# Last layer of a four-layer graph network: which operand of the dense product TensorE holds, and how the strips are loaded

## The reference

```python
def _L3_gnn_ref(emb, edge_weight, row, col, num_layers):
    w = edge_weight[:, None]
    X = emb
    for _ in range(num_layers):              # 3
        msgs = w * X[col]
        X = jax.ops.segment_sum(msgs, row, num_segments=n)
    return X
...
x = _layernorm(x + _L3_gnn_ref(x, edge_weight, src, dst, 3), axis=-1)
```

## Time and profile before

| | us |
|---|---|
| median of 3 runs | 4498.11 (4493.66 to 4520.53) |
| the profiled execution | 4511.84 |
| its span, first to last instruction | 4510.1 |
| mean granted clock of TensorE | 0.903 of full |
| last layer, from its first load to the end | 4060.9 to 4510.1 |

### The profile page before, as it was taken

One profiled execution on the slowest core, in us unless ns is written; L12 is line 12 of the kernel. 1 busy time (PEld: TensorE's weight loads), 2 busy tenths in 40 slices (PEclk: granted clock), 3 DMA queues, 4 the chain that ended last, 5 costly groups with the idle time before them and its releaser, 6 DMA issues. The chain is left out here.

```text
span 4510.1 us, 106688 instructions
## 1 busy us (share of the span) xinstructions
PE 3111.8 (69%) x28819; PEld 1977.5 (44%) x28820; DVE 2512.7 (56%) x7841; ACT 1512.7 (34%) x3455; POOL 2049.9 (45%) x3286
## 2 busy tenths in 40 slices
PE   2420000257777777777777799999999449988998
PEld 1100000046666666666665355555555325542222
DVE  7842212466666666666665698989998514440000
ACT  0011111124333333333333577777777301100000
POOL 1047777534444444444442588888888400000000
PEclk9999999879888888888887798988998779998999
DMA  9101111134444443334341110110101450008673
GB/s 375 58 14 23 22 23 22 20 107 136 136 135 135 135 135 121 127 120 129 120 136 70 28 27 26 26 27 26 28 26 26 85 106 0 0 0 367 287 303 136
DMA packets 190491, 431.03 MB, mean 96 GB/s; under 512 B 32352, under 2 KB 143066, under 8 KB 177274
## 3 DMA queue, kind: packets, MB, share of 16 engines
q1 hardware_dynamic: 156988, 365.02, 23.1%
q0 software_dynamic: 32816, 61.65, 6.1%
q10 hardware_dynamic: 520, 2.80, 0.2%
HBM read 227.36 MB, written 136.86 MB: 81 GB/s over the span
## 5 line engine op out<-in xcount | busy, mean ns | idle before, releaser
L208 POOL DMA_INDIRECT sorted_edges<-s_record,s_index x400 | 476.1, 1190 | 370.6 <-issue 362.1
L809 POOL TENSOR_TENSOR e_part<-e_rest,e_part 128x256 bf16<-128x256 f32 x202 | 133.2, 659 | 785.6 <-ACT e_part L851 785.6
L1016 DVE TENSOR_TENSOR e_strip<-e_p_aw,e_strip 128x256 f32 x804 | 334.9, 417 | 269.3 <-issue 199.7
L1347 POOL TENSOR_SCALAR m_oh<-m_iotab,m_rec 128x128 bf16<-128x128 bf16 x812 | 474.5, 600 | 0.1
L2068 PE MATMUL r_p_o<-r_W,r_X 128*32 128x512 f32 (+1 forms) x1050 | 408.3, 549 | 41.4 <-DMA r_W<-dense_strips 39.2
L803 POOL TENSOR_TENSOR e_ohw<-e_oh,e_rec 128x512 bf16<-128x512 bf16 x408 | 420.7, 1059 | 10.5 <-DVE e_oh L993 7.8
L1793 PE MATMUL q_p_s<-q_A,q_g 128*96 128x512 bf16 (+1 forms) x1750 | 349.5, 357 | 102.8 <-DMA q_A<-dense_strips 101.5
L259 PE MATMUL s_p_t<-s_ident,s_oh_src 125*128 125x125 f16 x100 | 21.2, 284 | 504.3 <-issue 259.0
L1000 DVE TENSOR_SCALAR e_ohw<-e_p_iota,e_rec 128x128 bf16<-128x128 f32 x816 | 327.7, 403 | 0.0
L842 ACT ACTIVATE e_hid<-e_p_hid,e_b 128x512 f32<-128x512 f32 x204 | 140.3, 688 | 557.8 <-PE e_p_hid L901 557.8
L1793 PEld LDWEIGHTS q_p_s<-q_A,q_g 128*96 128x96 bf16 x1750 | 197.7, 123 | 235.0 <-issue 105.8
(11 more groups left out here) (309 smaller groups left out, 7423.0 us busy)
## 6 DMA issues: line engine op xcount, KB each, us to landing
r_W<-dense_strips SPq DMA_DIRECT2D x18, 6400.0 KB, 17.7
e_strip<-e_zeros SPq DMA_DIRECT2D x26, 3200.0 KB, 13.8
dense_strips<-e_strip SPq DMA_DIRECT2D x25, 3200.0 KB
sorted_edges<-s_neg SPq DMA_DIRECT2D x1, 40560.0 KB, 161.8
e_rec<-sorted_edges POOLq DMA_DIRECT2D x208, 130.0 KB, 2.4
m_rec<-sorted_edges SPq DMA_DIRECT2D x208, 130.0 KB, 2.1
q_A<-dense_strips POOLq DMA_DIRECT2D x25, 800.0 KB, 46.2
sorted_edges<-s_record,s_index POOLq DMA_INDIRECT x400
```

The source lines that it names most:

```text
L208: pool.indirect_dma_start(dram["edges"], bass.IndirectOffsetOnAxis(ap=index[s][:, c:c + 1], axis=0), record[s][:, c, :], None).then_inc(s_ ...
L1016: i = V.tensor_tensor(at, p_aw[u][:, v, :].rearrange("p (k c) -> p k c", k=2), at, ALU.add)
L1347: i = g.tensor_scalar(oh[s][:, t, :], iotab[:, :], rec[s][:, t, CDST:CDST + 1], None, ALU.is_equal)
```

## The change

The operands of the product change places. A 128 by 128 block of a strip becomes TensorE's weights, and X, 32 columns, moves; the result comes out with the target nodes in the partitions, as X needs it. ScalarE's copies, the transposes, `r_Y` and its copy to X go; VectorE copies each group of four finished blocks from PSUM (seven tiles `r_p_o`, one for each group) right into the other of two X tiles. In step n+1 the matmul of source block d = 0, 4, 8, ... of the first strip waits for the copy of the group that it reads.

The buffers hold single strips now. Ten of the 25 strips (those with b % 5 of 2 or 4) have a buffer each and are loaded once, the other 15 pass through a ring of three in every step. TensorE waits for each strip alone. The loops over steps are written out on TensorE, VectorE and SP, and the flags go.

```diff
-        SL = 3
-        W = [sb(f"W{k}", [P, 4, NB, P]) for k in range(SL)] + [sb(f"W{SL}", [P, width[-1], NB, P])]
-        X = sb("X", [P, NB, D])
-        Y = sb("Y", [P, NB, D])
+        stays = [b % 5 in (2, 4) for b in range(NB)]
+        RING = 3
+        held = [sb(f"held{k}", [P, NB, P]) for k in range(sum(stays))]
+        ring = [sb(f"ring{k}", [P, NB, P]) for k in range(RING)]
+        passing = [b for b in range(NB) if not stays[b]]
+        order = [(n, b) for n in range(STEPS3) for b in passing]
+        X = [sb(f"X{k}", [P, NB, D]) for k in range(2)]
...
         def _(sp):
-            for f in primed:
-                sp.sem_inc(f.semaphore, 1)
-            with sp.Fori(1, STEPS3 + 1) as n:
-                for c in range(CH):
-                    last_user(sp, summed, slot, c, n)
-                    sp.dma_start(W[slot[c]][:, :, :, :].rearrange("p b d k -> p b (d k)"),
...
+            for n in range(STEPS3):
+                for b in range(NB):
+                    if stays[b] and n:
+                        continue
+                    strip, strip_in, _ = strip_of(n, b)
+                    if not stays[b]:
+                        i = order.index((n, b))
+                        if i >= RING:
+                            n0, b0 = order[i - RING]
+                            sp.wait_ge(multiplied, n0 * NB + b0 + 1)
+                    sp.dma_start(strip[:, :, :].rearrange("p d k -> p (d k)"), dram["strips"][b, :, 1, :]).then_inc(strip_in, 16)
...
         def _(pe):
...
-                    for d in range(NB):
-                        m = nc.tensor.matmul(p_o[c % 3][:, 0:width[c] * P], X[:, d, :],
-                                             W[slot[c]][:, :, d, :], start=(d == 0), stop=(d == NB - 1))
-                    summed[c].set_by(m)
-                    if c:
-                        turn(c - 1)
-                turn(CH - 1)
+            for n in range(STEPS3):
+                for b in range(NB):
+                    strip, strip_in, count = strip_of(n, b)
+                    pe.wait_ge(strip_in, count)
                     for d in range(NB):
+                        if b == 0 and d % 4 == 0:
+                            if n:
+                                pe.wait_ge(gathered, (n - 1) * CH + d // 4 + 1)
+                            elif d == 0:
+                                pe.wait_ge(started, 1)
+                        m = nc.tensor.matmul(p_o[b // 4][:, b % 4, :], strip[:, d, :], X[n % 2][:, d, :],
+                                             start=(d == 0), stop=(d == NB - 1), skip_group_check=True)
+                    m.then_inc(multiplied, 1)
...
-                    turned[c].after(dve, n)
-                    gathered[c].set_by(V.tensor_copy(Y[:, 4 * c:4 * c + width[c], :], p_t[c % 2][:, 0:width[c], :]))
-                gathered[CH - 1].after(dve, n)
-                renewed.set_by(V.tensor_copy(X[:, :, :], Y[:, :, :]))
+                    dve.wait_ge(multiplied, n * NB + 4 * c + width[c])
+                    V.tensor_copy(X[1 - n % 2][:, 4 * c:4 * c + width[c], :], p_o[c][:, 0:width[c], :]).then_inc(gathered, 1)
```

More of the change, by code:

```diff
@@ L1999, in sem @@
             return used[-1]
[L2001 to L2007, removed]
+        x = keep["x"]
         CH = -(-NB // 4)
         width = [min(4, NB - 4 * c) for c in range(CH)]
-        SL = 3
-        W = [sb(f"W{k}", [P, 4, NB, P]) for k in range(SL)] + [sb(f"W{SL}", [P, width[-1], NB, P])]
-        slot = [c % SL for c in range(CH - 1)] + [SL]
@@ L2013, in layer3_phase @@
-        loads = [slot.count(k) for k in range(SL + 1)]
-        X = sb("X", [P, NB, D])
-        Y = sb("Y", [P, NB, D])
-        sT = [sb(f"sT{k}", [D, 4 * P]) for k in range(2)]
+        stays = [b % 5 in (2, 4) for b in range(NB)]
[4 more added lines that the diff above has]
+        order = [(n, b) for n in range(STEPS3) for b in passing]
@@ L2017, in layer3_phase @@
+        X = [sb(f"X{k}", [P, NB, D]) for k in range(2)]
         std = sb("std", [P, 4, NB])
-        p_o = [ctx.enter_context(nc.psum_tensor(f"r_p_o{k}", [D, 512], F32)) for k in range(3)]
-        p_t = [ctx.enter_context(nc.psum_tensor(f"r_p_t{k}", [P, 4, D], F32)) for k in range(2)]
-        arrived = [sem(f"arrived{k}") for k in range(SL + 1)]
+        p_o = [ctx.enter_context(nc.psum_tensor(f"r_p_o{c}", [P, 4, D], F32)) for c in range(CH)]
+        held_in = [sem(f"held_in{k}") for k in range(len(held))]
@@ L2021, in layer3_phase @@
+        ring_in = [sem(f"ring_in{k}") for k in range(RING)]
         started, s_v, s_std, s_root, final, stored = sem("started"), sem("v"), sem("std"), sem("root"), sem("final"), sem("stored")
-        summed, copied, turned, gathered = flags("summed", CH), flags("copied", CH), flags("turned", CH), flags("gathered", CH)
-        renewed, passed = flags("renewed", 1)[0], sem("passed")
+        multiplied, gathered = sem("multiplied"), sem("gathered")
         block = ctx.enter_context(nc.Block())
[L2026 to L2032, removed]
@@ L2034, in layer3_phase, with strip_of @@
-        two, three = [c % 2 for c in range(CH)], [c % 3 for c in range(CH)]
+        def strip_of(n, b):
+            if stays[b]:
+                k = sum(stays[:b])
+                return held[k], held_in[k], 16
+            i = order.index((n, b))
+            return ring[i % RING], ring_in[i % RING], 16 * (i // RING + 1)
         @block.sync
         def _(sp):
-            for f in primed:
-                sp.sem_inc(f.semaphore, 1)
-            with sp.Fori(1, STEPS3 + 1) as n:
-                for c in range(CH):
-                    last_user(sp, summed, slot, c, n)
-                    sp.dma_start(W[slot[c]][:, :, :, :].rearrange("p b d k -> p b (d k)"),
-                                 dram["strips"][4 * c:4 * c + width[c], :, 1, :].rearrange("b p x -> p b x")
-                                 ).then_inc(arrived[slot[c]], 16)
+            for n in range(STEPS3):
[4 more added lines that the diff above has]
+                    if not stays[b]:
+                        i = order.index((n, b))
+                        if i >= RING:
+                            n0, b0 = order[i - RING]
+                            sp.wait_ge(multiplied, n0 * NB + b0 + 1)
+                    sp.dma_start(strip[:, :, :].rearrange("p d k -> p (d k)"), dram["strips"][b, :, 1, :]).then_inc(strip_in, 16)
@@ L2052, in _ @@
         def _(pe):
[L2053 to L2066, removed]
-                    for d in range(NB):
-                        m = nc.tensor.matmul(p_o[c % 3][:, 0:width[c] * P], X[:, d, :],
-                                             W[slot[c]][:, :, d, :], start=(d == 0), stop=(d == NB - 1))
-                    summed[c].set_by(m)
-                    if c:
-                        turn(c - 1)
-                turn(CH - 1)
+            for n in range(STEPS3):
+                for b in range(NB):
+                    strip, strip_in, count = strip_of(n, b)
+                    pe.wait_ge(strip_in, count)
+                    for d in range(NB):
+                        if b == 0 and d % 4 == 0:
[6 more added lines that the diff above has]
+                    m.then_inc(multiplied, 1)
         @block.scalar
         def _(act):
[L2077 to L2081, removed]
             act.wait_ge(s_std, 1)
@@ L2093, in link @@
                 dve.wait_ge(s_v, at[0])
-            V.tensor_copy(X[:, :, :], x[:, :, :]).then_inc(started, 1)
-            with dve.Fori(1, STEPS3 + 1) as n:
+            V.tensor_copy(X[0][:, :, :], x[:, :, :]).then_inc(started, 1)
+            for n in range(STEPS3):
                 for c in range(CH):
-                    turned[c].after(dve, n)
-                    gathered[c].set_by(V.tensor_copy(Y[:, 4 * c:4 * c + width[c], :], p_t[c % 2][:, 0:width[c], :]))
-                gathered[CH - 1].after(dve, n)
-                renewed.set_by(V.tensor_copy(X[:, :, :], Y[:, :, :]))
-            renewed.after(dve, STEPS3)
+                    dve.wait_ge(multiplied, n * NB + 4 * c + width[c])
+                    V.tensor_copy(X[1 - n % 2][:, 4 * c:4 * c + width[c], :], p_o[c][:, 0:width[c], :]).then_inc(gathered, 1)
+            dve.wait_ge(gathered, STEPS3 * CH)
+            Y, spare = X[STEPS3 % 2], X[1 - STEPS3 % 2]
             link(V.tensor_tensor(Y[:, :, :], Y[:, :, :], x[:, :, :], ALU.add))
-            layernorm(dve, V, link, x, Y, X, std, s_std, s_root)
+            layernorm(dve, V, link, x, Y, spare, std, s_std, s_root)
             dve.sem_inc(final, 1)
```

## The result

| | before | changed |
|---|---|---|
| median, us | 4495.89 (4 runs, 4486.66 to 4520.53) | 4851.37 (4 runs, 4834.09 to 4864.45) |
| ratio | | 1.0779, 95% interval 1.0724 to 1.0834 |
| ratio when timed again, more rounds | | 1.0805, 1.0764 to 1.0847 |
| span of the profiled execution, us | 4510.1 | 4832.4 |
| mean granted clock | 0.903 | 0.841 |

In the second timing one of the 23 executions of the kernel before took 11588.2 us at a mean clock of 0.574; it is left out of the ratio, the other 22 took 4475.59 to 4522.74 us.

The account below looks back on a forecast made before the run. TensorE's instruction rate was taken to bound the last layer. At the low clock 4066.8 + 799.9 + 1 + 0.4 + 12.3 = 4880.4, 370.3 above the old span; added to the median 4498.1 this gave 4868 us, range 4848 to 4900.

Parts of the forecast that it names:

- the price of a record: Last layer, TensorE: one matmul record costs about 0.111 us at the higher clock, 0.2133 at the lower, set by weight loading.
- First load: Start of the last layer: first strip lands after 7.7 us, TensorE starts at 4066.8 in place of 4080.1, gain 13.3 us.
- Stream: Last layer's 3750 TensorE records at 0.2133 us each, low clock: 799.9 us; 416 us at the high clock.
- Boundaries: TensorE's waits at the heads of 75 strips in the last layer: 0 to 0.1 us each, 1 us in all.
- From step to step: Between the last layer's steps: copies hide behind 48 records, so the 1.75 us wait goes, twice.
- Code: Reading the last layer's written-out matmuls, 1875 in place of 200: taken as 0, a few tens of us possible.
- End: After the last layer's stream: last record's way through the array and one small copy, 0.4 us.
- Which clock: Last layer: TensorE's granted clock stays at 0.50 from first record to last, though busy; chance 89%.
- The clock rising at 32 columns: Rival for the last layer: clock rises because all 128 rows take part; 4484 us, no change over 1%; chance 5%.
- the price of a transpose: Rival for the last layer: records cost 0.09 us each, as the transposes do; 4406 us; chance 3%.
- a clock going up and down: Rival for the last layer: half the time at each clock level; 4676 us; chance 3%.
- Everything up to 4059 stays: Phases ahead of the last layer: time unchanged, so the first load is issued at about 4059.1.

Follow-up runs that it names:

- move128: Changed kernel with 128 columns of X moving in place of 32, the extra products never read: 4495.62 us median, ratio 0.9978 to the kernel before.
- move32_warm: Changed kernel, 32 columns moving, with eight matmuls of 512 f32 columns put ahead of the first strip: 4867.89 us in one execution.

## Why the prediction was right in direction and cause, and high in its number

**What bounds, and the price of a record.** Right. 0.2133 us was forecast for the lower level, 800.22 / 3750 = 0.2134 measured; 0.111 for the higher, 0.1116 measured in move128. That the weight load sets the pace and that its time doubles at the lower level was read from three lines of other phases.

**The sum, term by term.** First load landed after 7.7 us forecast, 6.4 and 6.3 measured. Stream 799.9, measured 800.2. Boundaries 1, measured 0: in the second profile one chain piece holds all 3750 records. From step to step nothing, as forecast. Code nothing, as forecast, though nine times as many matmuls are written out. End 0.4, measured 0.24. From the first load to the final additions 809.0 was forecast, 806.9 and 806.8 were measured. Against 438.7 from the first flag before that is 368.2, where 370.3 was forecast.

**Which clock.** Right, and for the reason given. The doubt that I named (128 rows in place of 65 or 32) is settled by the changed kernel itself: 800 us of stream at 0.50. The sentence of the Trainium skill (TensorE: Matmul & The Clock Gate, "Why this matters for your kernels") that a continuously busy TensorE comes to the full rate fails here: PE and PEld were busy 270.00 of 270 us at 0.50.

**The rivals.** The clock rising at 32 columns, the price of a transpose, and a clock going up and down didn't happen. A stream whose level depends on where it begins does exist, at 64 columns; for 32 it isn't so (move32_warm).

**What failed: the premise "Everything up to 4059 stays", and with it the step from the profiled execution to the median and the allowance below.** The sum took the time ahead of the layer as one fixed number. In the profiled execution of the changed kernel the first load was issued at 4013.26, where 4059.1 was forecast: of the 48.0 us by which that profile lies below the sum (4880.4 and 4832.4), 45.8 lie ahead of the layer and 2.1 in it. The second layer's edge phase, 1012 us there and 1053 to 1054 in three other profiles, accounts for 41 of them. In the second profile of the changed kernel the first load was issued at 4056.11, in the six profiles of its variants between 4027.18 and 4056.80.

For the medians I had put the difference of the last layer onto the median before and allowed some 20 us below for scatter; the three times before, of which the lowest lay 4 us below their median, gave no hint of more. The ten executions of the changed kernel lie between 4834.09 and 4877.15, 43 us apart. The first four gave a median of 4851.37, 17 below my 4868 and only 3 above the lower end of my range, with one of the four outside it; the difference of the medians is 355.5 us where 370.3 was forecast and the layer itself gives 368.2. So the mis-sized term is the time ahead of the layer, put at no change: about 13 of those 15 us are there, and 2 in the layer. The ratio's middle, 1.0779, is below 4868 / 4498 = 1.0822, though its interval holds that. The second timing gave 4867.97, 368.0 above the median beside it, and a ratio of 1.0805. That the layer's 368 came back is the sum's merit; that the median met 4868 to the microsecond is luck, as the six executions behind it spread over 28 us. How large the difference of the medians is to better than some 15 us stays open, since the two intervals overlap; and why the clock stands lower for longer in some executions stays open too.

## What to carry to other kernels

Which operand TensorE holds is not only a matter of columns and instructions: a stream of many short moving operands can run without a gap and still be granted the lower clock (here 0.50 for 800 us), and then each weight load costs double (0.213 us in place of 0.111). Look in the trace for the nearest form and read its granted clock beside its price; if 32 columns move, hold the 32 columns instead and set neighbouring matmuls side by side in column groups. And when a stage is worked out well, don't narrow the range by it before you know how much the untouched stages differ from one execution to the next.

## What the runs showed that I had not expected

- 64 moving columns ran 800.28 us at 0.50 or 418.90 us at 1.00, by what TensorE did in the 10 us before (one execution of each). Work that was put ahead for nothing but the clock saved 381 us of the stream.
- Moving four times as many columns (move128) made the layer's stream 1.9 times faster, 421.94 us in place of 800.22.
- Four column groups of f32 matmuls ran 3.2 times as fast as one at a clock of 1.00, 0.034 against 0.110 us a record, although the two records of a matmul use the same columns.
- An unchanged phase of 9424 matmul records took 1012 or 1053 us, at a mean clock of 0.94 or 0.89, in executions of the same kernel.
